# Eight TensorE products per FFN chunk: the four 32-bit high products ahead of the four 16-bit low ones instead of in turn

## The reference, cut to what matters

```python
h = jnp.einsum('btd,hd->bth', x, absmean(W_fc))     # x: layer-normed, W_fc: 2048 x 512, ternary
h = jax.nn.gelu(h, approximate=False)
h = layernorm(h, ln_w, ln_b)
return jnp.einsum('bth,dh->btd', h, absmean(W_proj))   # W_proj: 512 x 2048, ternary
```

## Time and profile before

| | |
|---|---|
| median of three runs | 1549.47 us (1549.36 to 1549.59) |
| the profiled execution | 1549.63 us, of which span 1547.8 us |
| granted TensorE clock | 1.00 throughout |
| PE busy | 1527.7 us, 99% of the span |
| DVE, ACT, POOL busy | 1337.8, 1021.5, 1007.3 us |
| matmuls | 7744 |
| high products of L620 | 508; busy 243.9 us by the records |
| low products of L620 | 508; busy 198.6 us by the records |

### The profile page before, as it was taken

The page is one execution under the profiler, slowest core; times in us unless marked ns, Lnnn a source line. Parts: engine busy times, 40 slices in busy tenths (PEclk is TensorE's granted clock), DMA queues, the critical chain, the costliest instruction groups (busy, mean ns, idle before and its releaser), DMA issues.

```text
span 1547.8 us, 22931 instructions
## 1 busy us (share of the span) xinstructions
PE 1527.7 (99%) x7744; PEld 1174.8 (76%) x7744; DVE 1337.8 (86%) x1893; ACT 1021.5 (66%) x1688; POOL 1007.3 (65%) x1141
## 2 busy tenths in 40 slices
PE   9999999999999999999999999999999999999999
PEld 7877888888888888888888867676767666666766
DVE  8998999999899989999888888787878787787877
ACT  7988788898687897788987344444444444444354
POOL 6766657578867678686777655555655655565565
PEclk9999999999999999999999999999999999999999
DMA  4211312321311203122054631020302020211001
GB/s 170 76 40 64 111 46 90 123 69 62 123 65 61 68 28 119 43 85 95 22 177 143 211 117 41 20 90 0 110 1 89 21 89 21 64 45 53 16 15 41
DMA packets 73157, 113.20 MB, mean 73 GB/s; under 512 B 5193, under 2 KB 37961, under 8 KB 69970
## 3 DMA queue, kind: packets, MB, share of 16 engines
q1 hardware_dynamic: 72754, 111.21, 21.2%
q10 hardware_dynamic: 288, 0.52, 0.1%
HBM read 73.95 MB, written 37.77 MB: 72 GB/s over the span
## 4 chain that ended last, share of the span: by engine, by line
PE 51%; DVE 2%; ACT 1%; issue 0%; POOL 0%; DVEq 0%; ACTq 0%; POOLq 0%
PE ps L620 15%; PE ps L639 15%; PE ps L572 11%; PE ps L499 6%; PE ps L519 1%; PE ps L585 1%; PE ps L533 1%; PE ps L649 1%; PE ps L662 0%; DVE bnp L1132 0%; ACT H L876 0%; DVE yb L1112 0%; DVE H L1120 0%; ACT AH L880 0%; DVE H L1121 0%
## 5 line engine op out<-in xcount | busy, mean ns | idle before, releaser
L499 PE MATMUL ps<-AH,WH 128*128 128x512 f32 x896 | 366.9, 409 | 7.8 <-DVE H L1121 6.1
L499 PE MATMUL ps<-AL,WH 128*128 128x512 f32 x896 | 350.9, 392 | 0.0
L499 PE MATMUL ps<-AH,WL 128*128 128x512 f32 x896 | 349.5, 390 | 0.0
L1687 POOL TENSOR_TENSOR acq<-acq,sq 128x512 f32<-128x512 f32 x120 | 180.1, 1501 | 162.9 <-ACT sq L963 162.6
L1572 POOL TENSOR_TENSOR H<-H,yb 128x512 f32<-128x512 f32 x192 | 246.0, 1292 | 8.5 <-DVE yb L1112 1.3
L950 ACT ACTIVATE g<-ps 128x512 f32<-128x512 f32 x128 | 76.3, 596 | 259.4 <-PE ps L620 259.3
L1112 DVE TENSOR_TENSOR_SCAN yb<-ab,ps 128x512 f32<-128x512 f32 x192 | 232.0, 1209 | 15.0 <-POOL ab L1563 8.6
L837 ACT ACTIVATE yb<-ps,ncnd 128x512 f32<-128x512 f32 x224 | 158.3, 707 | 87.3 <-PE ps L499 84.3
L1307 DVE SCALAR_TENSOR_TENSOR gl<-g,wbcol,gh 128x512 fp32r<-128x512 f32 x118 | 125.3, 1062 | 98.7 <-ACT gh L960 98.5
L499 PEld LDWEIGHTS ps<-AH,WH 128*128 128x128 f32 x896 | 168.5, 188 | 46.4 <-DVE H L1121 8.7
L499 PEld LDWEIGHTS ps<-AL,WH 128*128 128x128 f32 x896 | 168.1, 188 | 37.1
(11 more groups left out here) (193 smaller groups left out, 3362.2 us busy)
## 6 DMA issues: line engine op xcount, KB each, us to landing
hs_scratch<-H SPq DMA_DIRECT2D x16, 1024.0 KB, 5.4
hc<-hs_scratch SPq DMA_DIRECT2D x32, 512.0 KB, 4.4
xr<-in_x SPq DMA_DIRECT2D x32, 256.0 KB, 4.5
out<-ob SPq DMA_DIRECT2D x32, 256.0 KB, 2.2
xbuf<-in_x SPq DMA_DIRECT2D x7, 1024.0 KB, 7.7
RAW<-in_wt SPq DMA_DIRECT2D x16, 256.0 KB, 6.5
stg<-in_fct SPq DMA_DIRECT2D x16, 256.0 KB, 3.2
stg<-in_pjt SPq DMA_DIRECT2D x16, 256.0 KB, 2.9
```

The source lines that it names most:

```text
L499: r = e.matmul(GATE[i % 3][:], w[:, q, m * 128:(m + 1) * 128], a[:, q, :], start=(n == 0), stop=(n == 11))
L1687: e.tensor_tensor(acq[b % 2][:], acq[b % 2][:], sq[:], ALU.add).then_inc(f_s2, 1)
```

## The change

In both functions the two loops change places: the pair (high, low) is now outside, the feature tile inside. A chunk's products come in the order high 0, 1, 2, 3, low 0, 1, 2, 3. Nothing is added or removed; first and last product keep the start and stop flags, and the waits and the signal stay where they were.

```diff
         def fc_of_first(t):
 
             n = 0
-            for q in range(KC):
-                for w, a in ((FC, xh), (FC16, xl16)):
+            for w, a in ((FC, xh), (FC16, xl16)):
+                for q in range(KC):
                     r = e.matmul(HIDDEN[0][:, t], w[q][:, 0:128], a[0][:, q, t], start=(n == 0), stop=(n == 7))
                     n += 1
             return r
```

## The result

The changed kernel takes 1541.28 us (1541.07 to 1541.62, four runs) where the kernel before takes 1549.53 (1549.36 to 1549.69): the ratio is 0.9947, 95% interval 0.993 to 0.9964, 8.25 us less. It is faster by more than the 0.2% of the text above, and lies outside the range given (1543.0 to 1550.4). The forecast of 1547.0 had the sign and a third of the size.

What follows compares the result with a forecast made beforehand. TensorE was taken to bound the kernel. A chunk's inside distances, 3 x 230 + 232.5 + 3 x 226 = 1600.5 ns against 1620, times 127 chunks gave -2.5 us, hence 1547.0 us; range 1543.0 to 1550.4.

Steps and rivals of the forecast that it cites:

- What bounds the kernel: Whole kernel: TensorE, busy 99%; only distances between ends of successive matmuls, times 127 first-projection chunks, set the change's time.
- a 16-bit product in turn is no shorter than a 32-bit one: First-projection chunk before the change: low products 232.5 ns, 32-bit neighbours 226 to 231; taking turns costs little.
- L-L = 226: Inside a first-projection chunk: distance from a low product's end to the next low product's end, taken as 226 ns.
- rival 2: First-projection chunk: low products behind low ones run at streaming pace, 213 to 222 ns; -5.9 us at 217; chance 0.21.
- H-H = 230: Inside a first-projection chunk: distance from a high product's end to the next high product's end, taken as 230 ns.
- L-H: Old first-projection chunk: distance from a low product's end to the next high product's end, three of them, taken as 230 ns.
- H-L: First-projection chunk: distance from a high product's end to the next low product's end, four before, one after, taken as 232.5 ns.
- the seven distances: Between ends of a first-projection chunk's eight products: 1620 ns before, 1600.5 after; entry and exit taken as unchanged.
- The mechanism: First-projection chunk: a low product's weight load gets cover behind another low product; chance 0.54 for both paces together.
- The rule against the change: Low products' weight loads: a load overlaps a matmul in flight only if its row group differs, so the gain would be nil.

Runs made afterwards that it cites:

- e2: Kernel before, with all eight products of a first-projection chunk 32-bit (the four high ones twice, low parts left out): 1542.67 us.
- e3: Kernel before, high and low still in turn, with 127 weight columns instead of 128 in the first projection's low products: 1539.40 us.
- e4: Changed kernel (grouped), with 127 weight columns instead of 128 in the first projection's low products: 1540.78 us.
- e9: Changed kernel, with the first projection's low products streaming the upper 16 bits of the 32-bit tile (step of two), low part left out: 1546.06 us.
- e7: Changed kernel, with the second projection's low products made 16-bit (weights read through their upper 16 bits) and grouped, four high then four low: 1548.94 us.
- e10: e7, with packed float8 copies, made by ACT, of 12 of 16 second-projection weight chunks for the low products: 1550.00 us.
- e5: Kernel before, with all eight products of a first-projection chunk 16-bit (the low ones twice, high parts left out): 1537.10 us.
- e1: Kernel before, with each first-projection chunk but the first in the order high, high, low, low, high, high, low, low: 1545.08 us.
- e12: e10 with lows first except in a batch's first chunk (old order), copies made after chunks 4 to 15, used from the second batch: 1542.32 us.

## Why the prediction was wrong

- **What bounds the kernel** was right: no wait moved, and all but 0.4 us of the gain are distances inside the chunks of L620.
- **That a 16-bit product in turn is no shorter than a 32-bit one** was read rightly, and what was concluded from it, that taking turns costs little, hid two things: the low product was paying 17 ns for a bare load (one that no matmul covers) and would be 11 ns cheaper than a 32-bit one without it. e2 shows the products in turn to be dearer than no 16-bit products. It is not the turns by themselves: with the long load they cost no more than groups (e3 against e4).
- **The step that failed is L-L = 226**, taken from the rows of L674 as "the nearest rows in format". It measured 215.7. The 0.22 us of L674 was read correctly, but those products stream the weights through a bfloat16 view with a step of two, and by e9 such a view makes 226 out of 216. The sum named the step and gave it to rival 2 as an argument; how the streamed operand lies should have ranked above its width of 16 bits. In 127 chunks this is 3 x 10.3 x 127 = 3.9 us of the 5.7 missed.
- **H-H = 230** was too dear: 227.8, 3 x 2.2 x 127 = 0.8 us. The bound was given (226), but the choice went to the distance of the same tile behind a low product, and a high product behind a long run of 32-bit ones takes less (last section). The start from 230 for L-H and 232.5 for H-L rounded the old chunk down to 1620 where it was 1625: another 0.6 us. The last 0.4 us are outside the seven distances.
- **The mechanism** was right: the load gets cover between low products, which had 0.54 for both paces together. Rival 2, with 0.21, is what happened; its price of -5.9 us was short mainly by the H-H term and by the rounding, and so the low end of the range, drawn at a distance of 215 but with H-H at 230, was too high. A range should take its terms' bounds together where they go the same way.
- **The rule against the change** did not hold: the loads of low products behind low ones ran 214 ns ahead of their matmuls. The Trainium skill (TensorE: Matmul & The Clock Gate, What overlaps and what doesn't) says that a load overlaps a matmul in flight only if its row group differs. The Trainium skill's back-to-back distance of 215.7 ns for warm matmuls of 512 columns (same page, Wait — 56ns, not 53.3ns?) is the measured L-L to the digit.

## What to carry to other kernels

When 16-bit and 32-bit matmuls share a stream, put the 16-bit ones next to each other: each one with a short load behind a 32-bit matmul pays 17 ns here. Look at the start of a weight load against the start of its own matmul: equal starts mean a bare load. A 16-bit product was worth 11 ns here with a packed streamed operand and nothing with the bfloat16 view of step two. Before an order is changed elsewhere, count what the old order gave time to (e7's evictions, e10's copies), and look at the unedited lines too.

## What the runs showed that was not expected

- A load of 128 16-bit columns (97 ns) costs more than one of 127 (138 ns) behind a 32-bit matmul: H-L 233 against 216. The shorter instruction is the dearer one.
- The distance of 512 columns is 216 ns for packed float16 (L620) and for packed float8 (215.8 in e10), and 226 for bfloat16 with a step of two or, at best, for 32-bit data.
- An edit elsewhere moves the 32-bit distances: L572, which no run edited, had a mean of 226.7 ns in e2, 229.5 in the changed kernel and 230.3 before. (The 232.2 of e5 is the half clock; without those eight it is 229.6.) Most of this goes by the place in the run of 32-bit products. From 896 us on, the mean distance of a 32-bit product by its place behind the last 16-bit product or transpose, distances over 260 ns left out (ns, how many):

| place | before | changed | e2 | all 14 traces |
|---|---|---|---|---|
| 1st to 4th | 231.3 (901) | 231.6 (595) | 232.2 (147) | 230.5 to 232.6 |
| 5th to 10th | 229.6 (678) | 228.5 (744) | 229.4 (222) | 227.7 to 230.0 |
| 11th and later | 227.0 (599) | 227.0 (836) | 226.8 (2317) | 226.2 to 227.1 |

So behind a change of kind the 32-bit products take some ns more each, until ten of them have gone by. It fits what the theory missed: H-H of 231.4 in e1, where it stands in the second place, the unedited lines of e2, where 2317 products stand in the 11th place or later, and the first projection of e7 and e12. Grouping gains by it too: 901 products stood in the first four places before, and 595 do in the changed kernel. Why the distances are long there is open, and the means of one place still differ by 1 to 2 ns between runs.
